# Prologue of a split-precision attention kernel: loads cut and reordered, the splitting of weights, values and tokens moved to other places and engines

## The reference

```python
q = rope(einsum('btm,mhd->bthd', x, w_aq)); k = rope(einsum('btm,mhd->bthd', x, w_ak))
v = einsum('btm,mhd->bthd', x, w_av)
s = einsum('bihd,bjhd->bhij', q, k) / 128 - 1e30 * (i < j)
r = einsum('bihd,hdm->bim', einsum('bhij,bjhd->bihd', softmax(s), v), w_ao)
x = layernorm(x + r)
h = silu(tlin(x, w1)) * tlin(x, w2);  h = gelu(tlin(h, h1));  h = gelu(tlin(h, h2))
x = layernorm(x + tlin(h, w3))
```

## Time and profile before

| what | value |
|---|---|
| median of 3 runs (lowest to highest) | 1034.44 us (1034.43 to 1035.41) |
| the profiled execution | 1034.38 us, span 1032.6 us |
| PE busy | 984.9 us, 95% of the span |
| DVE, ACT, POOL busy | 821.1, 593.4, 543.6 us |
| chain that ended last | PE 75%, DVE 11%, issue 6%, ACT 3%, POOL 2%, DMA 1% |

### The profile page before, as it was taken

How to read it: one execution, slowest core, us unless ns; L and a number is a source line. 1 busy time by engine, 2 the same in 40 slices (tenths; PEclk the granted TensorE clock), 3 DMA queues, 4 the chain that set the end, 5 groups by cost and what they waited for, 6 DMA issues and landing times.

```text
span 1032.6 us, 19696 instructions
## 1 busy us (share of the span) xinstructions
PE 984.9 (95%) x5648; PEld 856.0 (83%) x5648; DVE 821.1 (80%) x1795; ACT 593.4 (57%) x1263; POOL 543.6 (53%) x549
## 2 busy tenths in 40 slices
PE   2899999999999999999999999999989999999995
PEld 2688888888888898988889888888878888888884
DVE  5888888888888888888888888888866678586744
ACT  4566666666656666666666566665664252443521
POOL 4776677677766767677676767766670101000000
PEclk8799999999999999999999999999999999999998
DMA  8442323532222233222222322222300000000000
GB/s 287 153 136 63 71 61 81 174 92 62 53 67 75 61 77 96 63 51 62 65 67 70 74 62 52 62 61 62 113 1 1 1 1 21 1 20 0 1 21 21
DMA packets 33291, 66.16 MB, mean 64 GB/s; under 512 B 5456, under 2 KB 6992, under 8 KB 32208
## 3 DMA queue, kind: packets, MB, share of 16 engines
q1 hardware_dynamic: 30400, 58.62, 21.3%
q10 hardware_dynamic: 2832, 6.82, 1.8%
HBM read 24.26 MB, written 7.34 MB: 31 GB/s over the span
## 4 chain that ended last, share of the span: by engine, by line
PE 75%; DVE 11%; issue 6%; ACT 3%; POOL 2%; DMA 1%; DVEq 0%; SPq 0%; ACTq 0%; POOLq 0%
PE psum L327 26%; PE psum L989 17%; PE psum L423 9%; PE psum L413 5%; PE psum L410 5%; PE psum L414 4%; PE psum L964 4%; DVE neg_max L655 3%; POOL probs L762 2%; PE psum L1002 2%; DVE pT L671 2%; DVE by_sin L682 2%; ACT pT L567 1%; ACT probs L555 1%; DVE by_cos L684 1%
## 5 line engine op out<-in xcount | busy, mean ns | idle before, releaser
L762 POOL TENSOR_SCALAR probs<-probs,inv_sum 128x128 f32<-128x128 f32 (+7 forms) x256 | 191.2, 747 | 224.8 <-DVE inv_sum L661 224.4
L567 ACT ACTIVATE pT<-psum 128x512 fp32r<-128x512 f32 (+3 forms) x384 | 174.2, 490 | 134.7 <-PE psum L423 132.9
L327 PE MATMUL psum<-pT,vals 128*128 128x512 f32 (+3 forms) x1152 | 243.5, 351 | 1.0 <-DVE pT L671 1.0
L555 ACT ACTIVATE probs<-psum,neg_max 128x128 f32<-128x128 f32 (+7 forms) x256 | 190.3, 743 | 83.7 <-DVE neg_max L655 82.0
L671 DVE TENSOR_TENSOR pT<-psum,pT 128x512 fp32r<-128x512 f32 (+3 forms) x384 | 201.0, 551 | 30.4 <-ACT pT L567 26.4
L655 DVE TENSOR_REDUCE neg_max<-psum 128x1 f32<-128x128 f32 (+7 forms) x256 | 191.7, 749 | 26.5 <-PE psum L414 25.3
L327 PEld LDWEIGHTS psum<-pT,vals 128*128 128x128 f32 x1152 | 188.8, 190 | 23.8 <-DVE pT L671 1.2
L423 PE MATMUL psum<-ident,probs 128*128 128x128 f32 x1152 | 172.4, 276 | 8.4 <-POOL probs L762 6.3
L989 PE MATMUL psum<-hid,w 128*128 128x512 f32 x768 | 176.3, 390 | 0.0
L767 POOL TENSOR_TENSOR swapped<-by_cos,swapped 128x512 f32<-128x512 f32 x128 | 164.7, 1299 | 13.8 <-DMA swapped<-by_sin 13.8
L989 PEld LDWEIGHTS psum<-hid,w 128*128 128x128 f32 x768 | 143.7, 188 | 29.5
(11 more groups left out here) (85 smaller groups left out, 1129.7 us busy)
## 6 DMA issues: line engine op xcount, KB each, us to landing
swapped<-by_sin SPq DMA_DIRECT2D x256, 128.0 KB, 2.3
w_stage<-qk_split SPq DMA_DIRECT2D x30, 256.0 KB, 2.6
wv_stage<-v_split SPq DMA_DIRECT2D x15, 256.0 KB, 2.6
x_split<-ffn_raw ACTq DMA_DIRECT2D x2, 1024.0 KB, 5.2
ffn_raw<-g SPq DMA_DIRECT2D x2, 1024.0 KB, 8.0
x_moving<-x_split SPq DMA_DIRECT2D x2, 1024.0 KB, 5.0
out<-y SPq DMA_DIRECT2D x4, 512.0 KB, 2.6
raw_x<-xT SPq DMA_DIRECT2D x3, 512.0 KB, 11.2
```

Source lines behind the costliest of these rows:

```text
L327: ins = nc.tensor.matmul(out_ap, left[a], right[b], start=first and i == 0, stop=last and i == 2)
L555: nc.scalar.activation(probs[:, ib % 4, :width].rearrange("p (h c) -> p h c", h=halves), score_ps[:, ib % 2, :halves, :half], ACT.Exp, bia ...
L567: nc.scalar.activation(pT[chunk][:, 0, 4 * f:4 * f + n_blocks, (ib % 4) * P:(ib % 4 + 1) * P], bank("t", head[1], nth)[:, :n_blocks * P].r ...
L762: nc.gpsimd.tensor_scalar(p, p, inv_sum[:, n:n + 1], 1.0, ALU.mult, ALU.mult).then_inc(probs_ready[0], 1)
```

## The change

It touches the prologue and the tokens' splitting. In its parts:

- **Loads.** SP loads the weights of heads 0 and 1 alone, then half of the rope table, mask and identity. ACT's queue carries the tokens of batch 0, the other half of the rope table, the value and output weights, then the other heads' weights. The waits are split likewise (`qk_loaded[0]`, `qk_loaded[1]`, `rope_loaded[0]`, `rope_loaded[1]`, `masks_loaded`). The tokens of batches 1 to 3 go straight into `ffn_raw`, loaded after head 1's swaps.
- **Tokens.** They are split in halves of 512 columns. Batch 1's are split by ACT and DVE in steps 5 and 7 of head 1; those of batches 2 and 3 by ACT in steps 3 and 5 of heads 8 and 16 and by POOL in steps 0 and 1 of heads 9 and 17, into `x_moving` directly. `x_split` and its DMAs are gone. The feed-forward weights are loaded before batch 3 instead of before batch 1.
- **Values' weights.** Their eight matmuls stand in prologue step 3 instead of 1 and write PSUM banks 3 and 7; ACT splits them in two halves.
- **Low parts.** DVE makes the low parts of the values' weights and of the other heads' query weights after the maximum of block 1, and the low parts of the other heads' key weights at the end of step 0 of head 0. DVE takes over one rope sum (tile 1) and two low parts (tiles 0 and 1) of head 0 from POOL. The casts of mask and identity move from DVE to ACT.
- **Saving.** `save_weights` moves from ACT's queue to SP's, between the swaps of head 0 and those of head 1.
- **Swaps.** `by_sin` has four buffers instead of two, and each tile its own semaphore `swap_done`.

```diff
+X_STEPS = (5, 7)
+X_HIGH_STEPS, X_LOW_STEPS = (3, 5), (0, 1)
...
-            sp.dma_start(raw_w[:, 0], w_q).then_inc(qk_loaded, 16)
-            sp.dma_start(raw_w[:, 1], w_k).then_inc(qk_loaded, 16)
-            sp.dma_start(rope[:], rope_in).then_inc(consts_loaded, 16)
...
-            for b in range(1, B):
-                sp.dma_start(raw_x[:, b], xT[:, b * T:(b + 1) * T]).then_inc(x_loaded[b], 16)
...
+            first = slice(0, 2 * P)
+            sp.dma_start(raw_w[:, 0, first], w_q[:, first]).then_inc(qk_loaded[0], 16)
+            sp.dma_start(raw_w[:, 1, first], w_k[:, first]).then_inc(qk_loaded[0], 16)
+            sp.dma_start(rope[:, :, :BANK], rope_in[:, :, :BANK]).then_inc(rope_loaded[0], 16)
...
+            def save_weights():
+                for nth, (heads, parts) in enumerate(weight_parts):
+                    sp.wait_ge(qk_low, nth + 1)
+                    sp.dma_start(qk_split[heads].rearrange("h p k d -> p h k d"),
+                                 parts[:].bitcast(F32)).then_inc(w_saved, 16)
+                sp.wait_ge(vo_low, 2)
+                for part in range(2):
+                    sp.dma_start(v_split[:, :, part].rearrange("h p d -> p h d"),
...
+                            sp.dma_start(swapped[lo:lo + 64, j], by_sin[hi:hi + 64, j]).then_inc(
+                                swap_done[j][0], 16)
                     if q == 0 and first:
+                        save_weights()
                         stage_for_values()
 
             stage_pair(0, 0)
+            for b in range(1, B):
+                sp.dma_start(raw_x[b], xT[:, b * T:(b + 1) * T]).then_inc(x_loaded[b], 16)
             sp.wait_ge(w_saved, W_SAVED)
...
+            rest = slice(2 * P, H * P)
+            act.dma_start(raw_x[0], xT[:, :T]).then_inc(x_loaded[0], 16)
+            act.dma_start(rope[:, :, BANK:], rope_in[:, :, BANK:]).then_inc(rope_loaded[1], 16)
             act.dma_start(raw_w[:, 2], w_vT).then_inc(vo_loaded, 16)
             act.dma_start(raw_w[:, 3], w_o).then_inc(vo_loaded, 16)
+            act.dma_start(raw_w[:, 0, rest], w_q[:, rest]).then_inc(qk_loaded[1], 16)
+            act.dma_start(raw_w[:, 1, rest], w_k[:, rest]).then_inc(qk_loaded[1], 16)
...
+                if odd_of_batch(head, b) and b == 0 and s in X_STEPS:
+                    high_of_x(b + 1, X_STEPS.index(s))
+                if odd_of_batch(step_on(head, 1), b) and b > 0 and s in X_HIGH_STEPS:
+                    high_of_x(b + 1, X_HIGH_STEPS.index(s))
...
+                if before_first(head) and s == 2:
+                    second_sum()
+                if before_first(head) and s == NI - 1:
+                    for half in range(2):
+                        low_of_values(half)
+                    low_of_queries()
+                if is_first(head) and s == 0:
+                    low_of_keys()
```

More of the change, by code:

```diff
@@ L161, in run, with vo_ps @@
     taken = {b for j in range(NQK) for b in USES["qk", 2, j]}
-    vo_bank = next(b for b in range(PV_BANK) if not taken & {b, b + 1})
-    vo_ps = psum[:, vo_bank * BANK:(vo_bank + 2) * BANK]
+    VO_BANKS = (3, PV_BANK)
+    assert not taken & set(VO_BANKS)
+    def vo_ps(half):
+        return psum[:, VO_BANKS[half] * BANK:(VO_BANKS[half] + 1) * BANK]
     weight_parts = ((slice(0, 2), w_stage), (slice(2, H), qk_parts))
-    qk_loaded, vo_loaded, consts_loaded = sem("qk_loaded"), sem("vo_loaded"), sem("consts_loaded")
+    qk_loaded = [sem("qk_loaded0"), sem("qk_loaded1")]
+    vo_loaded, masks_loaded, rope_loaded = sem("vo_loaded"), sem("masks_loaded"), [sem("rope_loaded0"), sem("rope_loaded1")]
     x_loaded = [sem(f"x_loaded{b}") for b in range(B)]
@@ L290, in before_first, with odd_of_batch @@
         return isinstance(head[0], int) and head[0] < 0
+    def odd_of_batch(head, b):
+        return isinstance(head[0], int) and number(head) == H * b + 1 and b < B - 1
     def pair_exists(pair):
@@ L486, in step @@
                     pe.wait_ge(masks_ready, 1)
-                    pe.wait_ge(vo_low, 1)
+                if is_first(head) and s == 1:
+                    pe.wait_ge(vo_low, 2)
                 if exists(ahead):
@@ new lines, in first_low_of_weights, with low_of_queries, low_of_keys @@
+                for buffer in range(2):
+                    dve.sem_inc(w_staged[buffer][0], 16)
+            def low_of_queries():
+                heads, parts = weight_parts[1]
+                dve.wait_ge(qk_high, 3)
+                nc.vector.scalar_tensor_tensor(parts[:, :, QL], raw_of(0, heads), SCORE_SCALE,
+                                               parts[:, :, QH].bitcast(F32), ALU.mult, ALU.subtract)
+            def low_of_keys():
+                heads, parts = weight_parts[1]
+                dve.wait_ge(qk_high, 4)
+                nc.vector.tensor_tensor(parts[:, :, KL], raw_of(1, heads), parts[:, :, KH].bitcast(F32),
+                                        ALU.subtract).then_inc(qk_low, 1)
@@ L651, in negative_max, with low_of_values @@
+            def low_of_values(half):
+                part = slice(half * BANK, (half + 1) * BANK)
+                dve.wait_ge(vo_high, half + 1)
+                nc.vector.tensor_tensor(v_parts[:, 1, part], vo_ps(half), v_parts[:, 0, part].bitcast(F32),
+                                        ALU.subtract).then_inc(vo_low, 1)
+            for c in range(CHUNKS):
+                low_of_x(0, c)
+            first_low_of_weights()
             def negative_max(head, ib):
@@ L685, in rope_products, with second_sum, first_low @@
                                         ALU.mult).then_inc(cos_done[0], 1)
+            def second_sum():
+                wait_for_swap(dve, (0, 0), 1)
+                wait_for(dve, cos_done, (0, 0), 1)
+                wait_for(dve, rope_done, (0, 0), 0)
+                nc.vector.tensor_tensor(swapped[:, 1], by_cos[:, 1], swapped[:, 1], ALU.add).then_inc(rope_done[0], 1)
+            def first_low(j):
+                which, c = ROPE_TILES[j]
+                high, low = (qk[:, 0, which, part, c * BANK:(c + 1) * BANK] for part in range(2))
+                wait_for(dve, rope_high, (0, 0), j)
+                nc.vector.tensor_tensor(low, swapped[:, j], high.bitcast(F32), ALU.subtract).then_inc(rope_low[0], 1)
             def values_low(pair, nth):
```

178 lines of the change are left out of this document (80 added, 98 removed).

## The result

The changed kernel takes 1039.1 us, the median of 5 runs (1037.63 to 1039.33), against 1034.95 (1034.43 to 1035.41) for the kernel before in the same 5 rounds: ratio 1.0038, 95% interval 1.0026 to 1.0049. It is slower by 0.4%, 4.15 us by the medians. The profiled execution took 1039.33 us, the highest of the five; its span is 1037.5 us, 4.9 us more than that of the kernel before. What follows accounts for these 4.9 us, those of two single executions.

The account below looks back on a forecast made before the run. PE's waits in the prologue were taken as the bound. From 1034.38 us, 0.0 at the end of head 0's ramp and +0.4 in head 1 made 1034.8 us, range 1030.7 to 1037.4.

Parts of the forecast that it names:

- landed by then: Prologue: half of the rope table taken as landed by the time tile 0 is there, at 10.5 us.
- the queue: SP's queue in head 0: head 1's first swap waits behind the saves and lands at 37.6, shrinking the lead from 7.9 to 1.3.
- 7.8 us for 2.5 MB, and 0.65 each for `wv_stage` and the first tile's swap: SP's queue from 28.5 us: time for saves and swap, scaled from 9.3 us for 3.0 MB; swap lands at 37.6.
- the clock: End of head 0's ramp: PE idles 6 us, restarts at 1.2 GHz from 41.2 to 46 or 47; remaining lead spent, net 0.0.
- I charge 0.4: Head 1, steps 5 and 7: batch 1's splits each delay POOL's scaling by 0.3 to 0.9; 0.4 us charged, bounds 0 and 1.8.
- nothing, bound 0.6 in all: Heads 8 and 16: ACT's four copies of 0.63 lie ahead of exponentials that wait for maxima, so cost nothing, at most 0.6.
- the queue and the clock together overrun: Rival, head 0's ramp: swap lands after 38.9, sums end later than before and low clock adds; 1037.1 us, chance 0.20.
- The rival in which the swap passes the saves: Head 0's ramp: SP's transfers not held by those ahead, PE keeps its clock; 1030.9 us, chance 0.12.

Follow-up runs that it names:

- adding bytes: Changed kernel with the values' weights saved a second time, 1.0 MB more in SP's queue ahead of head 1's swaps: 1041.62 us, ratio 1.0061.
- the kernel without the late splits: Changed kernel without splitting the tokens of batches 2 and 3 (ACT's copies and POOL's subtractions left out): 1037.77 us, ratio 1.0029.
- the filled wait: Changed kernel with 36 needless PE matmuls of 512 columns ahead of the transposes of block 4 of head 0: 1038.14 us, ratio 1.0032.
- the later load: Changed kernel, largest save on ACT's queue, batch 1 split in head 0 but loaded by SP after head 0's swaps, batches 2 and 3 split in other steps: 1028.59 us.

## Why the prediction was wrong

The forecast was 1034.8 us, no change, and the range ended at 1037.4; the result is 1039.1. The chain of events was right. What failed is the sum: the landing of the swap was put 1.9 us too early, head 1's splits at 0.4 us instead of some 1.3, and the later batches' splits at nothing instead of 1.15.

**Right: the mechanism and its place.** First scores 19.1 forecast, 19.71 in the trace (the half rope table that was "landed by then" held DVE's first product until 11.42 instead of 10.5, and most of that was made up); first maximum 20.2 against 20.38; block 3 scaled at 30.5 against 30.41; the rest of the weights' save issued at 28.5 against 28.57. POOL waits in its order for a swap behind the saves, PE idles and restarts at the lower clock. Moving the saves, adding bytes and filling the wait each confirmed one link of this.

**Wrong in size: the queue.** The step "7.8 us for 2.5 MB, and 0.65 each for `wv_stage` and the first tile's swap" gave a landing at 37.6; the sums began at 39.57. The view of `v_split`, whose second save is the last of the 2.5 MB, has

```profile
L351 SPq DMA_DIRECT2D v_split<-v_parts x2: 544/893/1242, 29.0 to 29.6; - x2
DMA to landing us min/median/max: 6.7/7.3/7.9
```

so the last save landed at 37.5, 8.9 us after the first was issued: 1.1 us more than forecast. The forecast had scaled 9.3 us for 3.0 MB down to 2.5 MB as if all of it were bytes, and had taken the median of two landings for the later one. The swap then followed 2.0 us later instead of 1.3. What goes behind the saves moves more slowly. Two windows of the changed kernel, the last two columns being the DMA engines' busy share and GB/s:

```profile
30.00:36.00 6.00, 4.34 (x24) 3.60 (x23) 4.67 (x9) 1.39 (x4) 0.69 (x1) 1.00 1.06 389
37.00:39.50 2.50, 0.00 (x0) 0.00 (x0) 0.00 (x0) 0.00 (x0) 0.00 (x0) 0.82 1.04 278
```

The engines are full in both and move 389 and 278 GB/s. In the first they carry saves to DRAM, in the second mostly transfers from SBUF to SBUF; whether that or their smaller size and other shape is the reason was not tried. The lead at the end of the sums was forecast as 1.3 us and is -0.5 (42.05 against 41.59).

**About right: the clock.** Charged 1.3 us. From the end of the sums to block 6 the trace loses 1.2 us (0.5 late, then 1.6), that of the kernel without the late splits 0.6; the filled wait gives 1.3 there, and 1.0 by the medians. So the 1.6 us where 0.0 was forecast come from the queue, not from this charge.

**Wrong: "I charge 0.4" for head 1.** It costs 1.35. I had each of the two pieces delay POOL by 0.3 to 0.9 and then took much of it as covered by PE's other work. Nothing covered it: the distance went from 1.6 on entering head 1 to 2.22 after step 5 and 2.94 after step 7, 0.6 to 0.7 us for each piece. With the later load the head loses nothing, so the splits are the cause. The bound of 1.8 contained it.

**Wrong: "nothing, bound 0.6 in all" for the later batches.** ACT's copies in steps 3 and 5 of heads 8 and 16, with POOL's subtractions in heads 9 and 17, cost 0.58 and 0.59 (the marker's distance from head 7 to 9 and from 15 to 17), which leaving them out gave back. Of these, 0.43 and 0.42 are there at the markers of heads 8 and 16, before POOL's subtractions. With both copies in step 2 those two markers keep their distance (6.84 to 6.83 and 6.66 to 6.67), so in step 2 they are free, as the forecast had taken them to be in steps 3 and 5.

**Not foreseen: the seam.** 0.8 us come after head 31 with the same instructions. In the eleven traces the clock is at half there for 3.4 or for 6.8 us. From the marker of head 31 to the end it took 272.3 to 272.4 us in the three with 3.4 (the kernel before, all saves on ACT's queue, the filled wait) and 273.2 to 273.9 in the eight with 6.8. That the clock is the cause is read from this, not tried. Nor does it show that the change brings the longer stretch: there is one trace of each kernel, and the unprofiled runs of the kernel before spread alike, 1033.8 to 1034.3 us at a mean clock of 0.989 and 1034.55 to 1035.5 at 0.986. The cause stays open.

The account: 1.6 (ramp) + 1.35 + 1.15 + 0.8 = 4.9 us, the growth of the span; the medians grew by 4.15. That the terms close is no proof of each: the ramp alone differs by 0.7 us between executions. The rival "the queue and the clock together overrun" described the first term and put 1037.1 on it. Head 1 and the later batches, 0.4 in the sum, took 2.5 and carried the result beyond that, with the seam on top. The rival in which the swap passes the saves is refuted by the 2.7 us per MB.

The range had an error of its own. With its terms (saves issued at 29.4, queue 1 us slower, 1.3 for the clock, 1.8 in head 1) the slow end is 0.6 + 1.3 + 1.8 us behind, 1038.1 and not 1037.5. The measured median lies beyond that too. At the fast end the same terms leave 3.8 us at 41.59, not 3.3. And in the rival that passes the saves, PE's idle time of "little over 3 us" is not less than from 16.2 to 19, which is 2.8, so no row supports that it would keep its clock.

## What to carry to other kernels

A transfer that many wait for must not stand in a DMA queue behind bulk stores: one save of 1.5 MB moved to another engine's queue, which also let the saves behind it go out early, was worth 9.3 us here (1039.1 to 1029.8). A stall of the matrix engine must be priced with the restart at the lower clock behind it, 1.0 to 1.5 us on top here. Small operations moved into a dense loop are free only in front of a wait of their own engine that is longer than they are; put ahead of the exponential or the reciprocal that feeds the chain, an operation of 0.6 to 1.0 us cost 0.6 to 0.7 us in head 1.

## What the runs showed that I had not expected

With the DMA engines full, 278 GB/s were moved where most transfers went from SBUF to SBUF, 389 where they were stores to DRAM. The first loads are as tight: 0.5 MB more at the end of the other queue made head 0's swaps land in 3.4 instead of 2.3 us and the prologue 1.6 us longer. At the seam PE's clock was low for 3.4 us in three kernels' traces and for 6.8 us in eight. Up to the end of the ramp two executions of the same instructions differed by 0.7 us, most of it with the moment at which the clock rose.
